# Layer 2's scan pass: other units for the sums, y stores on SP's queue, copies of C in three lots

## What is computed

```
def step(state, inp):
    d, b, c, uu = inp
    dA = jnp.exp(d[..., None] * A_neg[:, None, :, :])
    state = dA * state + (d * uu)[..., None] * b[:, :, None, :]
    y = jnp.einsum('kbcn,kbn->kbc', state, c)
    return (state, y)
_, ys = jax.lax.scan(step, init, (d_t, B_t, C_t, u_t))
```

## Time and profile before

| | |
|---|---|
| median of 3 runs | 16748.27 us (16746.03 to 16751.82) |
| the profiled execution | 16740.79 us, span 16739.1 us |
| busy over the whole span | PE 79%, DVE 67%, ACT 51%, POOL 40% |
| scan pass of layer 2 | from 8540 to 15095 us of the span |
| granted PE clock, mean | 0.856 |

### The profile page before, as it was taken

The page is one execution under the profiler, slowest core; times in us unless marked ns, Lnnn a source line. Parts: engine busy times, 40 slices in busy tenths (PEclk is TensorE's granted clock), DMA queues, the critical chain, the costliest instruction groups (busy, mean ns, idle before and its releaser), DMA issues. The chain is left out here.

```text
span 16739.1 us, 371849 instructions
## 1 busy us (share of the span) xinstructions
PE 13258.6 (79%) x130080; PEld 8791.3 (53%) x130080; DVE 11153.8 (67%) x10439; ACT 8476.8 (51%) x15113; POOL 6761.1 (40%) x3199
## 2 busy tenths in 40 slices
PE   7889999899988965444657887888778878887799
PEld 5666666666666642221235555555455545554477
DVE  5666666666666655554568887888788878885532
ACT  4444444444444435445556666666666666662200
POOL 1000000000000003234368888888888888881100
PEclk9999999999999988776768888888888888886799
DMA  5222222222222226668599999999999998997611
GB/s 128 58 68 57 57 60 55 61 60 56 58 65 61 55 86 159 157 163 201 147 210 208 207 208 206 206 208 208 206 207 208 207 205 207 208 209 211 184 44 37
DMA packets 1861415, 2344.84 MB, mean 140 GB/s; under 512 B 1067492, under 2 KB 1757932, under 8 KB 1836012
## 3 DMA queue, kind: packets, MB, share of 16 engines
q1 hardware_dynamic: 1606124, 2120.92, 53.4%
q10 hardware_dynamic: 242816, 134.91, 4.0%
q0 software_dynamic: 12288, 86.71, 2.3%
HBM read 1814.60 MB, written 556.32 MB: 142 GB/s over the span
## 5 line engine op out<-in xcount | busy, mean ns | idle before, releaser
L1789 DVE TENSOR_TENSOR_SCAN L2.h<-L2.ps,L2.db 128x912 f32<-128x912 f32 x2688 | 5400.7, 2046 | 1181.3 <-ACT L2.db L1712 1068.1
L1601 POOL TENSOR_TENSOR L2.db<-L2.du,L2.bt 128x896 f32<-128x896 f32 x2688 | 5560.1, 2097 | 1068.7 <-ACT L2.du L1719 832.6
L1623 PE MATMUL L2.ps<-L2.dm,L2.wa 32*128 32x112 f32 x21504 | 2441.9, 326 | 503.4 <-DVE L2.h L1789 383.7
L1705 ACT ACTIVATE L2.ps<-L2.ps 128x896 f32<-128x896 f32 x2688 | 2440.9, 908 | 492.0 <-PE L2.ps L1623 440.3
L1645 PE MATMUL L2.ps<-L2.h,L2.cd 128*8 128x96 f32 x50176 | 2576.8, 362 | 79.9 <-ACT L2.ysum L1726 67.1
L1623 PEld LDWEIGHTS L2.ps<-L2.dm,L2.wa 32*128 32x128 f32 x21504 | 1898.5, 220 | 1306.4 <-DVE L2.h L1789 785.6
L1635 PE MATMUL L2.ps<-L2.few,L2.fan 8*128 8x448 f32 x2688 | 1603.3, 680 | 832.9 <-ACT L2.du L1719 826.7
L1645 PEld LDWEIGHTS L2.ps<-L2.h,L2.cd 128*8 128x8 f32 x50176 | 1435.6, 108 | 806.3 <-ACT L2.ysum L1726 236.1
L1726 ACT COPY L2.ysum<-L2.ps 128x384 f32<-128x384 f32 x1568 | 751.7, 479 | 771.1 <-PE L2.ps L1645 666.5
L314 POOL TENSOR_TENSOR L1.x_res<-L1.x_res,L1.ob 96x3136 f32 (+1 forms) x16 | 95.4, 5977 | 2583.9 <-ACT L1.qv L457 2583.9
L1635 PEld LDWEIGHTS L2.ps<-L2.few,L2.fan 8*128 8x128 f32 x2688 | 443.5, 205 | 1192.4 <-ACT L2.du L1719 861.7
(11 more groups left out here) (258 smaller groups left out, 21196.1 us busy)
## 6 DMA issues: line engine op xcount, KB each, us to landing
L2.du<-du SPq DMA_DIRECT2D x4032, 224.0 KB, 6.0
L2.dm<-d SPq DMA_DIRECT2D x896, 336.0 KB, 7.2
y<-L2.ysum ACTq DMA_DIRECT2D x896, 84.0 KB
L0.left<-table SPq DMA_DIRECT2D x48, 1176.0 KB
L0.right<-table SPq DMA_DIRECT2D x48, 1176.0 KB
L1.left<-table SPq DMA_DIRECT2D x48, 1176.0 KB
L1.right<-table SPq DMA_DIRECT2D x48, 1176.0 KB
du<-L2p.work SPq DMA_DIRECT2D x64, 784.0 KB, 7.8
```

The source lines that it names most:

```text
L1601: pool.tensor_tensor(db[:, n % RB, :, 2:ROW], du[:, n % RD, :].rearrange("p (c t) -> p c t", t=SPAN), row, ALU.mult)\
L1623: mm = pe.matmul(decays[n % RA][:, lo:lo + SPAN], wa[rows, u * QUAD + e, :], dm[rows, u * QUAD + e, :], start=True, stop=True)
L1705: act.activation(a, a, ACT.Exp).then_inc(a_ready, 1)
L1789: dve.tensor_tensor_scan(h[:, half, u * UNIT:(u + 1) * UNIT, :].rearrange("p c t -> p (c t)"), decays[n % RA], db[:, n % RB, :, :].rearran ...
```

## The change

The sums move from units 3 to 9 to units 2, 3, 5, 6, 7, 9 and 10, and the takes to the unit after each. The y stores move from ACT to SP: two DMAs at SP's unit 5 and two at unit 6 of the half after that in which the sums were taken, behind a wait for the last take; the last two halves are stored at the end. The eight copies of C are made after ACT's units 11, 12 and 13 (three, three, two) and not all after unit 11.

```
-        FIRST_FILL = 3
+        SUM_AT = (2, 3, 5, 6, 7, 9, 10)
...
+            def half_span(k, s, half, earlier, later, table):
+
+                fills = count(sp, k, s, 2 * FILLS, (half - 1) * FILLS)
...
+                    if 5 <= u <= 6 and earlier is not None:
+                        if u == 5:
+                            sp.wait_ge(sum_out, fills + 2)
+                            steady(sp)
+                        store_y(*earlier, half, range(2 * (u - 5), 2 * (u - 5) + 2))
...
+                if isinstance(s, int) and s == 0:
+                    earlier = (k - 1, NSPANS - 1) if k else None
+                else:
+                    earlier = (k, s - 1) if isinstance(s, int) else (k, sp.snap(s - 1))
...
+            for half in range(2):
+                sp.wait_ge(sum_out, (DIRS * HALVES - 1 + half) * FILLS + 2)
+                store_y(DIRS - 1, NSPANS - 1, half, range(4))
...
-                    f = u - FIRST_FILL
-                    if 0 <= f < FILLS and not first:
+                    if u in SUM_AT and not first:
+                        f = SUM_AT.index(u)
...
-            def make_cd(k, s, fills):
+            def make_cd(k, s, fills, batches):
 
-                act.wait_ge(cc_in, count(act, k, s, 16, 16))
-                act.wait_ge(sum_ready, fills + 2 * FILLS)
-                for b in range(BATCH):
+                if batches[0] == 0:
+                    act.wait_ge(cc_in, count(act, k, s, 16, 16))
+                    act.wait_ge(sum_ready, fills + FILLS)
+                for b in batches:
...
-                    f = u - FIRST_FILL - 1
-                    if 0 <= f < FILLS and not first:
+                    if u - 1 in SUM_AT and not first:
+                        f = SUM_AT.index(u - 1)
...
-                if not first:
-                    act.wait_ge(sum_out, before + (FILLS + 2))
-                    steady(act)
-                    if half:
-                        store_y(k, s, 0)
-                    elif begun:
-                        store_y(k - 1, NSPANS - 1, 1)
-                    else:
-                        store_y(k, act.snap(s - 1), 1)
-                if half == 0:
-                    make_cd(k, s, before)
+                    if UNITS - 1 <= n <= UNITS + 1:
+                        at = 3 * (n - UNITS + 1)
+                        make_cd(k, s, count(act, k, s, 2 * FILLS), range(at, min(at + 3, BATCH)))
```

More of the change, by code:

```diff
@@ L1525, in load_du, with store_y @@
                     sp.dma_start(du[:, slot, g * QUAD * SPAN:(g + 1) * QUAD * SPAN], src).then_inc(du_in[slot], 16)
-            def half_span(k, s, half, later, table):
+            def store_y(k, s, half, quarters):
+                for q in quarters:
+                    at = s * SPAN + SPAN // 4 * q
+                    if k % 2:
+                        at = at * -1 + (TOK - SPAN // 4)
+                    rows = slice(at, at + SPAN // 4) if isinstance(s, int) else bass.ds(at, SPAN // 4)
+                    place = y_dram[k, :, rows, half * HALF:(half + 1) * HALF]
+                    sp.dma_start(place, ysum[32 * q:32 * q + BATCH, :, :]).then_inc(y_stored[half], 16)
+            def half_span(k, s, half, earlier, later, table):
+                fills = count(sp, k, s, 2 * FILLS, (half - 1) * FILLS)
                 units = count(sp, k, s, 2 * UNITS, half * UNITS)
@@ L1562, in span @@
                     later = (k, s + 1) if isinstance(s, int) else (k, sp.snap(s + 1))
-                half_span(k, s, 0, (k, s), k if k and isinstance(s, int) and s == 0 else None)
-                half_span(k, s, 1, later, k + 1 if last and k + 1 < DIRS else None)
+                if isinstance(s, int) and s == 0:
+                    earlier = (k - 1, NSPANS - 1) if k else None
+                else:
+                    earlier = (k, s - 1) if isinstance(s, int) else (k, sp.snap(s - 1))
+                half_span(k, s, 0, earlier, (k, s), k if k and isinstance(s, int) and s == 0 else None)
+                half_span(k, s, 1, earlier, later, k + 1 if last and k + 1 < DIRS else None)
             sp.wait_ge(cleared, 1)
@@ L1767, in _ @@
                 take_sum(DIRS - 1, 1, f, (DIRS * HALVES - 1) * FILLS)
-            act.wait_ge(sum_out, DIRS * HALVES * FILLS + 2)
-            store_y(DIRS - 1, NSPANS - 1, 1)
         @block.vector
```

## The result

The changed kernel takes **17383.22 us** (median, 17370.62 to 17392.67), the kernel before 16749.89 us in the same comparison. The ratio is 1.0378, 95% interval 1.036 to 1.0396: **3.8% slower**, 633 us. The sign was forecast, the size was not: 16940 us were predicted, and the range ended at 17280. The profiled execution's span is 17368.9 us.

What follows compares the result with a forecast made beforehand. Scan pass bound by DVE waiting on ACT and PE, DMA close behind. Terms 20.75, 3.06, 6.0 and 0.3 gave 30.1 us a half against 29.26: +190 us on 16740.8, forecast 16940; own range 16780 to 17180, 8 in 10 16430 to 17280.

Steps and rivals of the forecast that it cites:

- a loop: Scan pass: first take through PE, POOL and SP's stores to the next half's first take; 30.1 us a half.
- landing: From the fourth y store on SP's queue to its arrival, which frees the next half's first take; 6.0 us.
- free gains: Copies of C: a 2.3 us burst every second half leaves the chain; new sum places: at most 1 us per half.
- the gains are real but vanish: Scan pass: everything freed on ACT and PE, 3.4 us per half on offer, turns into ACT's wait for the store.
- to the fourth store: SP's queue, from the first y store to the fourth, with unit 6's du pair between; 3.06 us.
- This takes none of the stretching seen now: SP's store issue: du pair counted at 1.5 us, without today's slowing (2.28 for 1.28); up to 1 us per store possible.
- late rival: SP's stores: stretching stays, half of it 2 us, arrival 6.0, clock 0.7; 32.5 us a half, 17475 us; chance 0.14.
- S to the first store: From the moment the first take may go, through PE and POOL's unit 10, to SP's first y store; 20.75 us.
- the clock: PE's first units after the stall may run at the 1.2 GHz level; 0 to 1.3 us, taken as 0.3.
- the DMA floor: Scan pass: at 230 GB/s a half's bytes take 26.3 us, limiting any gain to 663 us.
- the first term: From the moment the first take may go, through PE's sums and fan-outs, to POOL's unit 7; mean 7.1 us.

Runs made afterwards that it cites:

- two_ysum: The changed kernel with a ysum buffer for each half, so a take waits for the stores of two halves before; 16501.36 us, ratio 0.9851.
- lots: The kernel before with only the copies of C split into three groups (3, 3, 2); 16583.49 us, ratio 0.9898.
- sums: The kernel before with only the sums moved to units 2, 3, 5, 6, 7, 9 and 10; 16587.6 us, ratio 0.9901.
- act_stores: The changed kernel without the store move: y stores on ACT's queue after unit 11 as before; 16468.14 us, ratio 0.9831.
- stores: The kernel before with only the y stores moved to SP: sums at units 3 to 9, all C copies after unit 11; 17676.27 us, ratio 1.0557.
- early: The changed kernel with all four y stores back to back at SP's unit 5, ahead of its du loads; 16885.06 us, ratio 1.0084.
- two_spread: The changed kernel with two ysum buffers and the four stores one each at SP's units 5, 7, 9 and 11; 16009.0 us, ratio 0.9559.
- two_act: The changed kernel with two ysum buffers, stores on ACT's queue, one ahead of each of units 0 to 3 of the next half; 16287.59 us, ratio 0.9724.

## Why the prediction was right and wrong

**Right: what bounds the kernel, and that the change closes a loop.** The loop's order stood as forecast: take, fan copies, POOL's units 7 to 10, SP's unit 4, stores, landing. The gap moved from unit 12 to unit 3 of every half (6.6 to 6.7 us in the span shown, 4 to 6 forecast), the waits for "DMA y" went up, PE stands idle ahead of its second sum, POOL's waits for du shrank. two_ysum shows the cause: take away that wait and 882 us come back.

**Half right: lots and sums.** As free gains they were sized at up to 1.2 us and at most 1 us a half, and alone brought 0.75 each. But "the gains are real but vanish" is wrong for them: together they bring 284 us with the stores on ACT (act_stores) and 293 us with the stores on SP (stores against the change). What vanished is what the move itself frees on ACT; the move costs 915 to 927 us either way.

**Wrong: the term "to the fourth store".** The step that failed is "This takes none of the stretching seen now". The terms were 0.48, 0.6, 1.5 and 0.48 us, 3.06 in all. The profile has 5.2 to 5.55, because the du pair behind two stores is blocked for 3.3 to 3.7 us. That is +2.3 us a half, 224 x 2.3 = 515 us, more than the 443 us by which the forecast fell short. The price had been read from the earlier trace rows, where a pair took 2.28 us, and bounded at 1 us per store; the sum used zero. The only ground that the prediction gives stands with its late rival: one queue alone may not be stretched. It was, at all 222 pairs behind two stores, by 2.2 us at the median, twice what the earlier trace rows had shown. The landing was 4.8 to 5.0 us, 1.1 less than forecast. First store to take together were 9.06 us in the sum and 10.1 to 10.5 in the trace.

**Small: S to the first store.** 20.75 us and 0.3 for the clock were predicted; it is 21.2 and 21.35 in this span, and 21.5 on average over the pass. With the pass's means the errors are +0.5, +2.3 and -0.8 us a half, together the 2.0 us between 30.1 and 32.1. The shorter landing hid part of the missing term, which was luck.

**The case that came true.** The measured 32.05 us a half lies 0.45 below the late landing at 32.5, which had 0.14 of the chances and of which the range held only half. Its stretching of 2 us was close to the 2.3 measured; its landing of 6.0 us was too long. The Trainium skill, "DMA: Bandwidth & Descriptors", section "Queues, rings and completion order", says that a DMA engine consumes the descriptors of one row's ring in order and takes turns between rows, by which the store would wait behind the loads queued on its row. Landing on SP's row, 4.8 to 5.0 us, was in fact quicker than the 6.0 of the du loads before. It was no slower than on ACT's either: four stores in a row on ACT's queue (act_stores, the 13 takes that waited under 2 us) had the take 9.4 to 10.8 us after the first, four in a row on SP's (early) 9.2. The loads around them differ, so no run here tells whether turns between rows play a part. Nor did early, which put no loads between the stores, win more than 1.3 us of the way from first store to take.

**Wrong, but not decisive: the DMA floor.** 230 GB/s in the densest stretch was taken as the most that the engines give, 26.3 us a half. two_spread moves 234 GB/s over 5 ms and has 25.9 us a half. The densest stretch of a kernel with stalls shows what was asked for there.

**Clock.** Two stretches of the kernel after:

```profile
11446.00:11458.00 12.00, 9.29 (x128) 5.84 (x128) 11.62 (x7) 10.38 (x25) 11.79 (x7) 1.00 0.78 193
...
11462.00:11474.00 12.00, 6.46 (x104) 4.55 (x108) 4.66 (x3) 5.10 (x11) 5.48 (x3) 0.72 0.82 183
```

The granted clock is full (2.4 GHz) at the end of a half, up to 11458, and 0.72 on average in the stretch with the wait for y. PE was idle from 11461.2 to 11467.5. The clock stood at 0.50, the 1.2 GHz level, from 11465 to 11471, which takes in the first fan-out after the wait:

```profile
11469.14 1.11 PE L1657 MATMUL L2.ps<-L2.few,L2.fan 8*128 8x448 f32 x1
```

It took 1.11 us against 0.64. This is within the first term, 7.3 against 7.1 us.

## What to carry to other kernels

A store that has to land before a single buffer is written again is a part of the loop, whatever queue it stands on. Before it is moved, add up the way from the last write to the first reuse, and give the buffer a twin if there is memory: here the twin alone brought 882 us, and with the stores spread out as well the move went from +927 us to -580. When an issue is moved to a busy queue, its price is what the *next* issues on that queue are blocked for, and a stretched row in the trace of before should enter the sum, not only the range. Spread such issues out: with two buffers, one at a time among the loads instead of two pairs was worth 492 us.

## What the runs showed that was not expected

- A du load pair issued behind two stores of 84 KB takes 3.5 us of SP at the median of the pass, behind one store (two_spread) 1.8, and otherwise 1.3.
- Four stores in a row take 4.71 us to issue on SP's queue (early), and the take that needs them follows 4.5 us later.
- With two buffers and spread stores POOL is busy 95% of the time (4765 of 5000 us): its products are close to being the next limit.
- Stores of 384-byte pieces and of 10.5 KB runs differ by only 1.4 to 1.8 us in 10.
- The DMA engines gave 234 GB/s at a share of 0.95 in two_spread, and in two_act 222 GB/s with a share of 1.00.
